# Splitting the chunk pairs of a linear-attention stage into single chunks on TensorE

## The reference

```python
def step(carry, inp):
    S, Z = carry
    qi, ki, vi, gi = inp
    S = S + jnp.einsum('bhtd,bhte->bhde', ki, vi)
    Z = Z + ki.sum(axis=2)
    num = jnp.einsum('bhtd,bhde->bhte', qi, S)
    den = jnp.einsum('bhtd,bhd->bht', qi, Z)[..., None] + 1e-06
    return ((S, Z), gi * num / den)
_, out = lax.scan(step, (S0, Z0), (qc, kc, vc, gc))
```

## Time and profile before

| | us |
|---|---|
| median of 3 runs | 756.12 |
| lowest, highest | 754.96, 763.8 |
| the profiled execution's own time | 754.96 |
| its span, first to last instruction | 753.4 |
| PE, DVE, ACT, POOL busy in it | 651.9, 480.6, 333.8, 168.4 |

### The profile page before, as it was taken

One profiled execution on the slowest core, in us unless ns is written; L12 is line 12 of the kernel. 1 busy time (PEld: TensorE's weight loads), 2 busy tenths in 40 slices (PEclk: granted clock), 3 DMA queues, 4 the chain that ended last, 5 costly groups with the idle time before them and its releaser, 6 DMA issues.

```text
span 753.4 us, 10819 instructions
## 1 busy us (share of the span) xinstructions
PE 651.9 (87%) x4017; PEld 428.7 (57%) x4017; DVE 480.6 (64%) x975; ACT 333.8 (44%) x539; POOL 168.4 (22%) x222
## 2 busy tenths in 40 slices
PE   5857869999999967369999999587799999999996
PEld 4645567777777756235534434464454444378885
DVE  5897885666666279667887801576588887232223
ACT  4213343333333331415656686452265567843332
POOL 2352323555555319311000000000100001002222
PEclk9987979999999969579999999879799999999999
DMA  8940010000000000573000000016520000050001
GB/s 212 232 151 1 2 56 1 1 1 0 1 1 0 1 0 2 167 224 103 15 2 2 2 2 1 0 53 193 177 86 2 2 2 2 16 153 1 1 1 56
DMA packets 47040, 36.18 MB, mean 48 GB/s; under 512 B 16206, under 2 KB 44892, under 8 KB 46988
## 3 DMA queue, kind: packets, MB, share of 16 engines
q1 hardware_dynamic: 46988, 35.49, 16.0%
HBM read 27.94 MB, written 7.34 MB: 47 GB/s over the span
## 4 chain that ended last, share of the span: by engine, by line
PE 39%; issue 23%; POOL 12%; DVE 12%; SPq 7%; DMA 3%; ACT 3%; POOLq 0%; DVEq 0%; ACTq 0%
PE psum L779 8%; POOL it_lo L1575 8%; PE psum L742 8%; PE psum L765 8%; SPq L391 4%; POOL wd L1558 3%; DVE qk L1171 2%; SPq L328 2%; PE psum L483 2%; PE psum L437 2%; PE psum L768 2%; DMA parts_scratch<-parts 2%; PE psum L438 2%; PE psum L439 2%; PE psum L745 1%
## 5 line engine op out<-in xcount | busy, mean ns | idle before, releaser
L956 ACT ACTIVATE pt<-psum 128x1024 f32<-128x1024 f32 (+1 forms) x192 | 147.8, 811 | 101.5 <-PE psum L768 73.1
L1255 DVE TENSOR_REDUCE mx<-psum 128x1 f32<-128x512 f32 (+3 forms) x216 | 132.6, 665 | 17.4 <-PE psum L742 8.9
L742 PE MATMUL psum<-kr,qr 96*128 96x512 bf16 (+3 forms) x384 | 111.1, 339 | 16.8 <-DMA kr<-parts_scratch 13.4
L765 PE MATMUL psum<-qr,kr 99*128 99x512 bf16 (+3 forms) x384 | 99.7, 333 | 9.3 <-DMA qr<-m3T 7.9
L1575 POOL TENSOR_TENSOR it_lo<-it,it_hi 128x512 fp32r<-128x512 f32 x48 | 67.1, 1398 | 161.9 <-ACT it_hi L994 160.7
L742 PEld LDWEIGHTS psum<-kr,qr 96*128 96x128 bf16 x384 | 36.9, 100 | 80.3 <-DVE mx L1255 30.5
L779 PE MATMUL psum<-pt,vp 128*32 128x512 f32 (+3 forms) x768 | 81.7, 498 | 0.0
L437 PE MATMUL psum<-h_hi,wf_hi 128*128 128x512 f32 x192 | 78.1, 407 | 3.9 <-issue 3.9
L439 PE MATMUL psum<-h_hi,wf_lo 128*128 128x512 f32 x192 | 75.7, 394 | 0.0
L438 PE MATMUL psum<-h_lo,wf_hi 128*128 128x512 f32 x192 | 75.5, 393 | 0.0
L1601 POOL TENSOR_SCALAR m<-m 128x16 bf16<-128x16 f32 x16 | 4.1, 254 | 307.7 <-DVE m L1255 154.2
(11 more groups left out here) (194 smaller groups left out, 1158.5 us busy)
## 6 DMA issues: line engine op xcount, KB each, us to landing
parts_scratch<-parts SPq DMA_DIRECT2D x16, 384.0 KB, 3.4
qr<-parts_scratch SPq DMA_DIRECT2D x48, 128.0 KB, 2.6
kr<-parts_scratch SPq DMA_DIRECT2D x48, 128.0 KB, 2.7
wmod<-in_L_wmod SPq DMA_DIRECT2D x1, 1536.0 KB, 6.3
x<-in_L_attn_x SPq DMA_DIRECT2D x2, 512.0 KB, 4.3
wmod<-in_L_wmod SPq DMA_DIRECT2D x1, 1024.0 KB, 5.8
packed<-in_L_ffn_down_W_packed SPq DMA_DIRECT2D x1, 1024.0 KB, 11.0
nat<-in_L_ffn_W_in_base SPq DMA_DIRECT2D x8, 128.0 KB, 2.4
```

Source lines behind the costliest of these rows:

```text
L742: m = pe.matmul(b, qr[0:PARTS_ROWS, c, h, (qt - 4 * c) * P:(qt - 4 * c + 1) * P], kr[0:PARTS_ROWS, ch, h, 0:w], start=True, stop=not diag)
L765: m = pe.matmul(bank[4 + 2 * at[0] + j][:, 0:w], kr[0:PARTS_ROWS + 3, kt // 4, h, (kt % 4) * P:(kt % 4 + 1) * P], qr[0:PARTS_ROWS + 3, c, ...
L956: act.activation(pt[:, n % 4, :, 0:w], psum[:, b:b + 2, 0:w], ACT.Exp, scale=0.25).then_inc(S["ex"], 1)
L1255: dve.tensor_reduce(dst, bank[at[0]][:, 0:k * w].rearrange("p (k w) -> p k w", k=k), AX, ALU.max).then_inc(S["p1_mx"], 1)
```

## The change

`kv_pair(t)` and `out_pair(t)` become `kv_chunk(c)` and `out_chunk(c)`, each with the two calls of one chunk and its own semaphore step of 1. The waits become those of the chunk: the K/V of chunk c waits for the masking of chunk c - 3 (the same bank), the output of chunk c for the running sum of c. The loop goes over 16 chunks; before the output of chunk c stands the K/V of chunk c + 2. Transposes and modulation stay once per tile. The other engines' code is unchanged.

```diff
-            def kv_pair(t):
+            def kv_chunk(c):
+                t, r = divmod(c, 2)
+                rows = slice(CHUNK * r, CHUNK * (r + 1))
                 pe.wait_ge(S["el_f"], t + 1)
-                if t == 1:
+                if c == 3:
                     pe.wait_ge(S["cu"], 1)
-                elif t > 1:
-                    pe.wait_ge(S["kmd"], 2 * t - 2)
+                elif c > 3:
+                    pe.wait_ge(S["kmd"], c - 3)
                 for f in range(2):
-                    for r in range(2):
-                        rows = slice(CHUNK * r, CHUNK * (r + 1))
-                        m = pe.matmul(bank[KV_BANK[(2 * t + r) % 3]][:, f * VW:(f + 1) * VW],
-                                      qk[rows, t, D + f * P:D + (f + 1) * P], v1[rows, t, f, :], start=True, stop=True)
-                m.then_inc(S["kv"], 2)
-
-            def out_pair(t):
-                pe.wait_ge(S["cu"], 2 * t + 2)
+                    m = pe.matmul(bank[KV_BANK[c % 3]][:, f * VW:(f + 1) * VW],
+                                  qk[rows, t, D + f * P:D + (f + 1) * P], v1[rows, t, f, :], start=True, stop=True)
+                m.then_inc(S["kv"], 1)
+
+            def out_chunk(c):
+                t, r = divmod(c, 2)
+                rows = slice(CHUNK * r, CHUNK * (r + 1))
+                pe.wait_ge(S["cu"], c + 1)
                 pe.wait_ge(S["q_e"], t + 1)
-                if t >= 2:
+                if r == 0 and t >= 2:
                     pe.wait_ge(S["ca"], t - 1)
                 for f in range(2):
-                    for r in range(2):
-                        c = 2 * t + r
-                        rows = slice(CHUNK * r, CHUNK * (r + 1))
-                        m = pe.matmul(bank[4 + t % 2][rows, f * VW:(f + 1) * VW],
-                                      qT[:, f, c * CHUNK:(c + 1) * CHUNK], cum[:, c % 4, f, :], start=True, stop=True)
-                m.then_inc(S["oc"], 2)
+                    m = pe.matmul(bank[4 + t % 2][rows, f * VW:(f + 1) * VW],
+                                  qT[:, f, c * CHUNK:(c + 1) * CHUNK], cum[:, c % 4, f, :], start=True, stop=True)
+                m.then_inc(S["oc"], 1)
...
             q_transpose(0)
-            kv_pair(0)
-            for t in range(NT):
-                if t >= 2:
-
-                    if t == 2:
+            kv_chunk(0)
+            kv_chunk(1)
+            for c in range(16):
+                if c % 2 == 0 and c >= 4:
+
+                    if c == 4:
                         pe.wait_ge(S["ld_wmod1"], 16)
-                    m = modulation(wmod1, 1, 7, t - 2)
-                    if t == 7:
+                    m = modulation(wmod1, 1, 7, (c - 4) // 2)
+                    if c == 14:
                         m.then_inc(S["mod_mm"], 1)
-                if t + 1 < NT:
-                    q_transpose(t + 1)
-                    kv_pair(t + 1)
-                out_pair(t)
+                if c + 2 < 16:
+                    if c % 2 == 0:
+                        q_transpose(c // 2 + 1)
+                    kv_chunk(c + 2)
+                out_chunk(c)
```

## The result

The changed kernel takes 780.85 us (median of 4 runs, 778.22 to 781.37) against 755.54 for the kernel before (754.68 to 763.8, 4 runs). The ratio is 1.0301, 95% interval 1.0264 to 1.0337. It is slower by 25 us; 5 were forecast, and the range ended at 766.5. One of the four runs of the kernel before, 763.8, most likely belongs to a second group of times, which the experiments come back to. Sixteen executions of the changed kernel lie between 778.2 and 782.8.

The account below looks back on a forecast made before the run. DVE was taken to set the pace at 2.35 us per tile, with PE taking over at 3.35 after the change. +6.95 for the stage and -1.75 for the clock gave +5.2: 760.2, 761.0 for a median, range 757 to 766.5.

Parts of the forecast that it names:

- The pair's overlap on two halves of the array: K/V and output pair groups: two instructions share a slot, one per array half, so eight instructions take four slots.
- four slots for four instructions: New chunk groups: each as long as the old group of eight, 0.66 us for K/V and 0.61 for output.
- PE's take-over as the bound: Middle of the stage: PE's sum per tile goes from 2.08 to 3.35 us, 1.00 over DVE's 2.35.
- A: Rival on chunk groups: half as long as the old, tile needs 2.43 us, total 756 to 757; chance 0.12.
- B: Rival on group overlap: splitting costs PE less than its spare 0.27 us per tile, total 755.2, not slower; chance 0.04.
- C: Rival on weight loads: exposed, +14 to +16 us in all, total 770; its sign a period over 4; chance 0.04.
- the walk through the head: Stage's start: groups summed in order with the clock rising during output chunk 0; first denominators at 67.45 instead of 65.93.
- 6.95: Whole linear-attention stage of layer 0: it ends 6.95 us later, before the credit for the clock behind it.
- The clock behind the stage: Attention transposes after the stage: clock stays up, so they take half of 3.51 us, 1.75 less.
- Rival D: Behind the stage: as forecast, but clock falls as before or worse, +7 to +8.5, 762 to 764; 0.3 of the 0.77.
- the 0.70 us for chunk 1 in the head: K/V groups of chunks 0 and 1: the second adds 0.70 us, three slots, between bounds 0 and 0.91.
- The reference for the sum: Profiled execution of the kernel before, 754.96 us, to which +5.2 was added; the fastest of three shown.

Follow-up runs that it names:

- e5: Changed kernel plus 36 identity transposes in TensorE's wait ahead of the stage, so the clock is up at its begin: 757.27 us; ten more executions, median 757.81.
- e6: Kernel before plus 36 identity transposes in TensorE's wait ahead of the stage: median 752.94 us of four executions, ratio 0.9886.
- e9: Kernel before without the K/V and output calls of the odd chunks, so only one array half works: eight executions, 761.6 to 763.4 us.
- e4: Kernel before with each pair group cut in two by half of the heads, K/V and output in turn: 768.96 us; four more executions, 766.1 to 769.3.
- e3_adjacent: Changed kernel's chunk calls and semaphore steps, but K/V of both chunks, then outputs of both chunks: 763.16 us.
- e3_again: Kernel of e3_adjacent repeated in ten executions: five between 754.5 and 756.7 us, five between 762.1 and 764.5.
- e7: Changed kernel plus unread extra matmuls on the idle array half in output groups and even-chunk K/V groups: 760.17 us; repeated, six at 757.0 to 762.7, four at 775.6 to 781.5.

## Why the prediction was wrong

- The bound and the structure were right. The pair's overlap on two halves of the array, four slots for four instructions, and PE's take-over as the bound all stand: 3.34 us per tile at the full clock in e5 against 3.35 forecast, 0.66 and 0.60 for the groups against 0.66 and 0.61. DVE idles 0.91 us per tile there, about the forecast 1 us. Rivals A and B are out: a chunk's group is as long as a pair's. C is out too: no load is exposed in the 0.66. The sign stated for C, a period over 4 us, did come (6.08), but from the low clock: at the full clock the same groups have a period of 3.34.
- The step that failed is in the walk through the head: "about 0.85 with the clock rising in it, as it rose at 65.7 before". I took the granted clock as given for the whole stage and let only the work change. It did not rise, and each of the following groups cost up to twice as much: 6.07 us per tile instead of 3.35. Five tiles at 6.07 instead of 3.35, and tile 1 at 5.22 instead of 2.88, make 15.9 of the 17.1 us by which the stage was longer than forecast (24.0 against 6.95). With the clock raised beforehand (e5) the same stage lasts 27.2 us (60.51 to 87.67) instead of 46.1, so 19 of the 24 us are the clock's and 5 the split's. Against e6, whose stage also begins at the full clock and lasts 21.0 us (63.06 to 84.09), the split costs 6.1, where 6.95 were forecast. The forecast gave being over 2% slower a chance of 0.04, and only by way of C; it came by a way that no rival had priced.
- The clock behind the stage was forecast to stay up (-1.75). In the changed kernel it was down all along, and the transposes took 3.65. At the full clock that step was right: in e5 PE idled 1.13 us once behind the last group, the clock stayed at 1.00, and the transposes took 1.94.
- Rival D had the right sign but priced only the stretch behind the stage, at most 8.5 us in all. A rival with the whole stage at the low level could be worked out from the earlier trace rows: 2 x 1.21 + 2 x 1.10 + 0.59 for a tile, and the modulation. That is 5.2 us even without the modulation, against a forecast period of 3.35 with it.
- Neighbouring chunks of different halves overlap fully, over a semaphore step: the 0.70 us for chunk 1 in the head should have been 0, its lower bound.
- The reference for the sum was itself one of two outcomes. The time 754.96 is of an execution in which the clock rose; the 763.8 among the runs shown was the hint of the other. I read it as scatter.

The page "TensorE: Matmul & The Clock Gate" of the Trainium skill, Part 1, says that the clock is held back by default and that activity releases it. The trace of the kernel before agrees: the clock is 0.50 behind PE's wait of 11.16 us, and it rises at 65.7, after PE has been at work since 60.86. The trace of the changed kernel does not bear it out in so plain a form: the clock stayed at 0.50 through 45.60 us in which the profile shows PE busy for 44.99.

## What to carry to other kernels

Before regrouping small matmuls, ask of each group what part of the array it fills, and price the stage at both clock levels: a group order that looks equally busy may no longer raise the clock, and then the stage can take nearly twice as long (46.1 us here against 27.2). Where PE waits ahead of a stage with thinly filled groups, spare matmuls placed in that wait can bring the clock up for the stage. They cost next to nothing as long as they end with the wait: the stage began 0.52 us after the start of DVE's modulation copy without them, and 0.25 to 0.83 us after it in the four traces with them. The clock may fall again at the next wait, as in e6. Where one kernel's times fall into two clusters, look at the mean granted clock of each execution first.

## What the hardware showed unexpectedly

- Rising and holding differ. Half-filled groups never raised the clock (0 of 16 executions of the changed kernel, 0 of 8 of e9), and held it in 11 of 11 when it was up at the start. Where there is no trace, this is by the time and the mean clock.
- Filling may not be all: full groups cut in two, with the changes of shape of the changed kernel (five per tile instead of three), did not raise it in any of 5 (e4), which chance could still explain; full groups as before did in somewhat over half (25 of 43 of the kernel before, 5 of 11 of e3_adjacent and e3_again). Filling three of the changed kernel's four chunk groups per tile raised it in 7 of 11. What of the engine's work the chip counts was not measured here, and why one execution of the same kernel rises and another does not is open.
- Calls on the idle half of the array cost no time: e7's output groups took 0.61 us with twice the instructions.
